# Last stages of layers 0 and 3: the sum over scan directions done band by band, with the norm, gate and projection of a band behind it

## What is computed

```python
# y: the four directions, each put back in the order of the pixels; D_skip weighs the input u
y = y_dir0 + y_dir1 + y_dir2 + y_dir3 + u * D_skip.sum(directions)
mu  = mean(y, over the 192 channels);  var = var(y, over the 192 channels)
y = (y - mu) * rsqrt(var + 1e-5) * ln_gamma + ln_beta
y = y * z                                   # z: the gate, computed earlier in the layer
x = x + y @ out_proj                        # 192 -> 96 channels, for each pixel
```

## Time and profile before

| what | value |
|---|---|
| median of 3 runs | 27758.6 us (27747.02 to 27776.92) |
| the profiled execution | 27776.42 us |
| its span in the trace | 27774.6 us |
| last stage of layer 0, sums (first to last, DVE) | 6959.6 to 7155.0 us |
| last stage of layer 0, steps (first matmul to last add) | 7155.1 to 7425.1 us |
| last stage of layer 3, sums | 27304.6 to 27500.0 us |
| last stage of layer 3, steps | 27500.1 to 27768.3 us |

### The profile page before, as it was taken

One profiled execution on the slowest core, in us unless ns is written; L12 is line 12 of the kernel. 1 busy time (PEld: TensorE's weight loads), 2 busy tenths in 40 slices (PEclk: granted clock), 3 DMA queues, 4 the chain that ended last, 5 costly groups with the idle time before them and its releaser, 6 DMA issues. The chain is left out here.

```text
span 27774.6 us, 412813 instructions
## 1 busy us (share of the span) xinstructions
PE 24946.7 (90%) x140112; PEld 9147.8 (33%) x140112; DVE 24955.1 (90%) x16019; ACT 14695.6 (53%) x19970; POOL 22628.6 (81%) x10100
## 2 busy tenths in 40 slices
PE   8989999999567999999987899999995899999996
PEld 3333333333233333333334333333332433333332
DVE  2489999999569999999986899999997799999997
ACT  1265555555267555555514655555552755555552
POOL 0179999999047999999971899999990599999992
PEclk9999999999677999999968999999997999999998
DMA  2242212221455212221266422212216622222224
GB/s 87 106 141 50 50 41 50 50 50 38 157 201 162 50 40 50 50 50 40 50 228 232 120 50 50 48 42 50 50 49 222 227 44 47 50 50 44 47 50 149
DMA packets 1121664, 2338.91 MB, mean 84 GB/s; under 512 B 98430, under 2 KB 609409, under 8 KB 1110893
## 3 DMA queue, kind: packets, MB, share of 16 engines
q1 hardware_dynamic: 1117748, 2309.42, 30.5%
q10 hardware_dynamic: 1728, 1.70, 0.0%
HBM read 1330.16 MB, written 980.58 MB: 83 GB/s over the span
## 5 line engine op out<-in xcount | busy, mean ns | idle before, releaser
L1598 POOL TENSOR_TENSOR scan_hc<-scan_bc,scan_h 128x1024 f32<-128x1024 f32 x6912 | 16131.4, 2384 | 135.7 <-PE scan_p_y L1710 72.1
L1786 DVE TENSOR_TENSOR_SCAN scan_h<-scan_da,scan_state,scan_dbu 128x1024 f32<-128x1024 f32 x6912 | 15948.4, 2332 | 38.6 <-POOL scan_dbu L1583 30.0
L1651 ACT ACTIVATE scan_da<-scan_da,scan_a_cur 128x1024 f32<-128x1024 f32 x6912 | 7521.7, 1088 | 6189.1 <-PE scan_da L1686 6188.7
L1686 PE MATMUL scan_da<-scan_dd,scan_ssel 32*128 32x512 f32 x27648 | 7870.4, 646 | 756.6 <-DVE scan_h L1786 40.8
L1686 PE MATMUL scan_p_du<-scan_dd,scan_ssel 32*128 32x512 f32 x27648 | 7906.8, 647 | 212.0 <-DMA scan_bc<-bc_d 110.0
L1773 DVE TENSOR_TENSOR scan_dbu<-scan_p_du,scan_bc 128x1024 f32<-128x1024 f32 x4752 | 5682.4, 1196 | 219.5 <-PE scan_p_du L1686 213.2
L1583 POOL TENSOR_TENSOR scan_dbu<-scan_bc,scan_dus 128x1024 f32<-128x1024 f32 x2160 | 5150.8, 2385 | 56.5 <-ACT scan_dus L1625 56.5
L1710 PE MATMUL scan_p_y<-scan_hc,scan_rsel 128*32 128x256 f32 x55296 | 4444.9, 393 | 0.0
L1694 PEld LDWEIGHTS scan_p_y<-scan_nought,scan_ssel 128*128 128x128 f32 x13824 | 2067.5, 189 | 4977.2 <-issue 3592.6
L1630 ACT ACTIVATE scan_state<-scan_h,scan_a_cur 128x1 f32<-128x1 f32 x6912 | 2036.9, 295 | 2734.3 <-DVE scan_h L1786 2610.6
L1686 PEld LDWEIGHTS scan_p_du<-scan_dd,scan_ssel 32*128 32x128 f32 x27648 | 2116.4, 185 | 4087.8 <-DVE scan_dbu L1773 3811.4
(11 more groups left out here) (225 smaller groups left out, 13731.3 us busy)
## 6 DMA issues: line engine op xcount, KB each, us to landing
scan_bc<-bc_d SPq DMA_DIRECT2D x576, 512.0 KB, 12.1
du_d<-prep_useq SPq DMA_DIRECT2D x384, 576.0 KB, 4.2
delta_d<-prep_delta SPq DMA_DIRECT2D x384, 576.0 KB, 4.7
y_d<-scan_y SPq DMA_DIRECT2D x576, 384.0 KB, 5.1
scan_dd<-delta_d SPq DMA_DIRECT2D x1136, 192.0 KB, 4.8
scan_dd<-du_d SPq DMA_DIRECT2D x1136, 192.0 KB, 6.5
fin_y<-y_d SPq DMA_DIRECT2D x288, 576.0 KB, 5.6
xs_d<-proj_xs_o SPq DMA_DIRECT2D x96, 588.0 KB, 3.3
```

What stands on the lines that cost most here:

```text
L1598: nc.gpsimd.tensor_tensor(hc[:, u % HC_SLOTS, :], c, h[:, u % H_SLOTS, :], ALU.mult).then_inc(hc_ready, 1)
L1651: nc.scalar.activation(da[u % DELTA_BANKS][:], da[u % DELTA_BANKS][:], ACT.Exp, scale=a_cur[:, slot(u)[0], u % UNITS:u % UNITS + 1]).then_ ...
L1686: return nc.tensor.matmul(dst[:, half * H:(half + 1) * H], ssel[rows, i, :], dd[rows, s, m, j, :], start=True, stop=True)
L1786: nc.vector.tensor_tensor_scan(h[:, v % H_SLOTS, :], da[v % DELTA_BANKS][:], dbu[:, v % DBU_SLOTS, :], state[:, v % UNITS:v % UNITS + 1], ...
```

## The change

Only `merge_finish_ln` is touched. The pieces are put in another order, and the steps run among them.

- `local` are the directions whose piece covers 12 whole lines of the image (a band: 1152 pixels of each tile); `whole` are those that walk by columns. In layer 0 all four are local. In layer 3 two are local and two whole.
- The pieces of the whole directions come first (`FIRST`: none in layer 0, 48 in layer 3). The local pieces follow band by band: in layer 0 there are `BAND` = 12 to a band, in layer 3 `BAND` = 6. There are 8 bands and 3 steps to a band (`PER_BAND`), so a turn of the DVE queue holds `TURN` = 4 pieces in layer 0 and 2 in layer 3.
- In turn t DVE adds the pieces of that turn, and then does `gate(s-2)`, `invert(s-1)`, `add(s-3)` with s = t - `LAG`, `LAG` = 3. PE no longer waits for all sums: before `centre_y` of every third step it waits for the band.
- SP issues, in each turn, the store, the loads of x and z, in every third turn of layer 0 a band of u, and then waits for each of the turn's pieces to be added in order to load the piece four further on.
- In layer 0 u is loaded and weighted in 8 bands of all three tiles (three ACT instructions of 1152 pixels each), two bands ahead; in layer 3 by tiles as before. The constants are loaded after the second load of u, ahead of all z and x; in layer 0 DVE waits for them before its first piece.
- Buffers: pieces 4 (were 6), z 3 (were 4), x 4 (were 6); the buffers of the steps have memory of their own.

```diff
-        DEEP = 4
-        X_DEEP = 6
+        DEEP = 3
+        X_DEEP = 4
...
-        Y_DEEP = 6
+        Y_DEEP = 4
...
+        whole = [k for k in range(DIRS) if walks[k][0] == "col"]
+        local = [k for k in range(DIRS) if walks[k][0] != "col"]
+        FIRST = [(m, k, c) for m in range(TILES) for k in whole for c in range(CHUNKS)]
+        BAND = TILES * len(local)
+        PIECES = FIRST + [(m, k, CHUNKS - 1 - b if walks[k][1] else b) for b in range(CHUNKS) for m in range(TILES) for k in local]
+        ALL = len(PIECES)
+        PER_BAND = DW // N
+        TURN = BAND // PER_BAND
+        LAG = 3
...
                 load_u(1)
-                for n in range(ALL - Y_DEEP):
-
-                    sp.wait_ge(added, (n + 1) * PAIRS + ONE)
-                    load_piece(n + Y_DEEP)
-                    if n == PER // 2:
-                        load_u(2)
...
+                for n in range(len(FIRST)):
+                    load_after(n)
+                    if n == CHUNKS:
+                        load_u(2)
                 for s in range(DEEP):
                     load_z(s)
                 for s in range(X_DEEP):
                     load_x(s)
...
+                for t in range(STEPS + 2 * LAG + 1):
+                    if t >= 2 * LAG + 1:
+                        store(t - 2 * LAG - 1)
+                    v = t - 2 * LAG - 2 + X_DEEP
                     if X_DEEP <= v < STEPS:
 
                         sp.wait_ge(stored[v % X_DEEP], 16 * (v // X_DEEP) + ONE)
                         load_x(v)
+                    v = t - 2 * LAG + DEEP
+                    if DEEP <= v < STEPS:
+
+                        sp.wait_ge(gated, (v - DEEP + 1) * TILES + ONE)
+                        load_z(v)
+                    if not whole and t % PER_BAND == 0 and t // PER_BAND + 2 < CHUNKS:
+                        load_u(t // PER_BAND + 2)
+                    for n in turn_pieces(t):
+                        load_after(n)
...
                 t.wait_ge(consts, 16 * 5 + ONE)
-                t.wait_ge(added, ALL * PAIRS + ONE)
                 for s in range(STEPS + 3):
...
                     if s < STEPS:
+                        if s % PER_BAND == 0:
+                            t.wait_ge(added, (len(FIRST) + (s // PER_BAND + 1) * BAND) * PAIRS + ONE)
                         centre_y(s)
...
                     if s >= 1:
                         deviation(s - 1)
+                    if not whole and s % PER_BAND == 0 and s // PER_BAND + 2 < CHUNKS:
+                        weigh(s // PER_BAND + 2)
                     if s < STEPS:
                         square(s)
...
+                for n in range(len(FIRST)):
+                    sum_piece(n)
                 d.wait_ge(consts, 16 * 5 + ONE)
-                for s in range(STEPS + 3):
+                for t in range(STEPS + 2 * LAG):
+                    for n in turn_pieces(t):
+                        sum_piece(n)
+                    s = t - LAG
                     if 0 <= s - 2 < STEPS:
                         gate(s - 2)
                     if 0 <= s - 1 < STEPS:
                         invert(s - 1)
```

More of the change, by code:

```diff
@@ L2149, in merge_finish_ln @@
         dskip_loaded = ph.sem("dskip_loaded")
-        u_loaded = [ph.sem(f"u_loaded{m}") for m in range(TILES)]
         piece_loaded = [ph.sem(f"piece_loaded{j}") for j in range(Y_DEEP)]
@@ L2156, in merge_finish_ln, with turn_pieces @@
         PAIRS = 2 if walks[0][0] == "window" or walks[0][2] == "snake" else 1
[L2157 to L2163, removed]
+        whole = [k for k in range(DIRS) if walks[k][0] == "col"]
[6 more added lines that the diff above has]
+        TURN = BAND // PER_BAND
+        U_PARTS = TILES if whole else CHUNKS
+        u_loaded = [ph.sem(f"u_loaded{i}") for i in range(U_PARTS)]
+        LAG = 3
+        def turn_pieces(t):
+            at = len(FIRST) + t * TURN
+            return range(at, min(at + TURN, ALL))
         z = ph.sb("z", [P, DEEP, TILES, N])
@@ L2171, in merge_finish_ln @@
         gamma = ph.sb("gamma", [P, P])
[L2173 to L2177, removed]
+        yc = ph.sb("yc", [P, 3, TILES, N])
+        sq = ph.sb("sq", [P, TILES, N])
+        yn = ph.sb("yn", [P, TILES, N])
+        t_ = [ph.sb(f"t{i}", [P, TILES, N]) for i in range(2)]
         sd = ph.sb("sd", [P, N])
@@ L2204, in load_piece, with load_u, load_after, load_z @@
                 def load_piece(n):
-                    m, k, c = where(n)
+                    m, k, c = PIECES[n]
                     at = (k * CHUNKS + c) * DW
                     sp.dma_start(y[:, n % Y_DEEP, :], y_d[:, m, at:at + DW]).then_inc(piece_loaded[n % Y_DEEP], 16)
-                def load_u(m):
-                    sp.dma_start(acc[:, m, :], u_d[:, m, :]).then_inc(u_loaded[m], 16)
+                def load_u(i):
+                    if whole:
+                        sp.dma_start(acc[:, i, :], u_d[:, i, :]).then_inc(u_loaded[i], 16)
+                    else:
+                        sp.dma_start(acc[:, :, i * DW:(i + 1) * DW], u_d[:, :, i * DW:(i + 1) * DW]).then_inc(u_loaded[i], 16)
+                def load_after(n):
+                    if n + Y_DEEP < ALL:
+                        sp.wait_ge(added, (n + 1) * PAIRS + ONE)
+                        load_piece(n + Y_DEEP)
+                def load_z(s):
+                    sp.dma_start(z[:, s % DEEP], z_d[:, :, s * N:(s + 1) * N]).then_inc(z_loaded[s % DEEP], 16)
+                def load_x(s):
+                    sp.dma_start(x[:, s % X_DEEP], x_d[:, :, s * N:(s + 1) * N].rearrange("b c n -> c b n")).then_inc(x_loaded[s % X_DEEP], 16)
+                def store(s):
+                    sp.wait_ge(out_ready, s + 1 + ONE)
+                    sp.dma_start(out_d[:, :, s * N:(s + 1) * N].rearrange("b c n -> c b n"),
+                                 x[:, s % X_DEEP]).then_inc(stored[s % X_DEEP], 16)
                 sp.dma_start(dskip[:], w["dskip"]).then_inc(dskip_loaded, 16)
@@ L2326, in square, with weigh @@
                     a.wait_ge(var_done, s + ONE)
-                    nc.scalar.activation(sq, yc[:, s % 3], ACT.Square).then_inc(squared, 1)
+                    nc.scalar.activation(sq[:], yc[:, s % 3], ACT.Square).then_inc(squared, 1)
+                def weigh(i):
+                    a.wait_ge(u_loaded[i], 16 + ONE)
+                    if whole:
+                        nc.scalar.activation(acc[:, i, :], acc[:, i, :], ACT.Copy, scale=dsum[:, i:i + 1]).then_inc(skip, 1)
+                    else:
+                        for m in range(TILES):
+                            own = acc[:, m, i * DW:(i + 1) * DW]
+                            nc.scalar.activation(own, own, ACT.Copy, scale=dsum[:, m:m + 1]).then_inc(skip, 1)
                 a.wait_ge(dsum_ready, 1 + ONE)
-                for m in range(TILES):
-                    a.wait_ge(u_loaded[m], 16 + ONE)
-                    nc.scalar.activation(acc[:, m, :], acc[:, m, :], ACT.Copy, scale=dsum[:, m:m + 1]).then_inc(skip, 1)
+                for i in range(TILES if whole else 2):
+                    weigh(i)
                 a.wait_ge(eps_set, 1 + ONE)
@@ L2351, in gate @@
                     d.wait_ge(gated, s * TILES + ONE)
-                    nc.vector.tensor_tensor(yn, yc[:, s % 3], p_r[:, :, 0:N], ALU.mult).then_inc(scaled, 1)
+                    nc.vector.tensor_tensor(yn[:], yc[:, s % 3], p_r[:, :, 0:N], ALU.mult).then_inc(scaled, 1)
                     d.wait_ge(scaled, s + 1 + ONE)
@@ L2369, in _, with sum_piece @@
                 nc.vector.tensor_reduce(dsum[:], dskip[:], mybir.AxisListType.X, ALU.add).then_inc(dsum_ready, 1)
-                for n in range(ALL):
-                    m, k, c = where(n)
+                def sum_piece(n):
+                    m, k, c = PIECES[n]
                     d.wait_ge(piece_loaded[n % Y_DEEP], (n // Y_DEEP + 1) * 16 + ONE)
-                    if n % PER == 0:
-                        d.wait_ge(skip, m + 1 + ONE)
+                    d.wait_ge(skip, m + 1 + (0 if whole else n // BAND * TILES) + ONE)
                     d.wait_ge(added, n * PAIRS + ONE)
```

4 lines of the change are left out of this document (removed).

## The result

The changed kernel takes 27612.9 us (median of 5 runs, 27607.63 to 27639.58) against 27762.16 us for the kernel before (5 runs): ratio 0.9943, 95% interval 0.9932 to 0.9955. That is 149 us less, where 156 were forecast. The forecast time was 27602, the range 27572 to 27667.

The account below looks back on a forecast made before the run. DVE would set layer 0's turn (14.1 us), the PE and ACT circle layer 3's step (10.35 us). Gains of 102 and 54 us sum to 156, against the median 27758.6 giving 27602 us, range 27572 to 27667.

Parts of the forecast that it names:

- DVE sets layer 0's turn: Layer 0's turns: DVE's sums 7.62 plus step work 6.47 make 14.1 us, over the PE circle's 10.35.
- Layer 0's fill: Start of layer 0: constants at 17.2 us, fifth piece at 33.7 (wait 8.9), turn 4 ends at 67.7.
- The 2.8 us for the short rows of z and x: Layer 0's start: extra transfer time before the fifth piece, as these rows go at 4.1 us per 1.18 MB.
- Layer 0's drain: Layer 0 after the last reciprocal at 333.7 us: 1.7, two circles (20.7), then 28.9 to last add at 385.0.
- from here PE sets the pace again: Layer 0 after `invert(19)`: `centre_y(21)` 1.7 us later, `centre_y(23)` two circles (20.7) on, last add 28.9 behind.
- rival 1: Layer 0's PE stays at 1.2 GHz, circle 17.1 us, 53 us lost over 18 turns (27655); chance 0.08.
- against it: Layer 0's PE clock: a slow turn has 3.7 us of idle to hide it; at the low rate no idle is left.
- rival 2: Transfers bound layer 0: each turn costs 16.1 us, 18 turns give back 36 us (27638); chance 0.06.
- The 12.7 us of the working: Layer 0's transfers for four pieces, a step and a third of a u band: 12.7 of 14.1 us, covered tightly.
- rival 3: Sums don't fit layer 3's loop: 2.92 us added to every circle, turns 3 to 23, lose 61 us (27663); chance 0.03.
- Layer 3's fill: Layer 3's start: column pieces 2.41 us each, waits 7.8 in FIRST, band 0 done at 163.0 us instead of 217.4.
- rival 4: SP's queue holds pieces back in both layers: 8.7 us a turn, 339 us, 182 slower in all (27941); chance 0.05.

Follow-up runs that it names:

- e2: Changed kernel with each step's reciprocal done twice on DVE, the first into a spare tile: 27696.98 us.
- e8: Changed kernel with loads reordered as in e6, plus the reciprocal root made on ACT (logarithm, exponential) instead of ACT's root and DVE's reciprocal: 27529.45 us, ratio 0.9913 to kernel before.
- e5: Changed kernel with 12 unread matmuls of 128 columns in PE's idle time ahead of each spread of layer 0 (steps 1 to 19): 27599.65 us.
- e9: The kernel of e6 again, timed in rounds against the kernel before: 27591.63 us, ratio 0.9935.
- e3: Kernel before the change with each step's reciprocal done twice on DVE: 27767.58 us.
- e4: Changed kernel with each turn's store one turn earlier in SP's queue, so SP waits for DVE's add before issuing that turn's piece loads: 27769.51 us.
- e6: Changed kernel with constants, first z and x behind the first pieces, layer 3's u in quarter tiles, layer 0's u bands later, two waits moved: 27589.48 us.

## Why the prediction was right, point by point

- **DVE sets layer 0's turn:** shown by the gapless DVE, by e2 (+2.4 us a turn for +2.5 us of work) and by e8 (-2.4 where nothing else waits). The turn is 13.8 us, not 14.1: `add` takes 0.89 us behind a reciprocal, not 0.95, and the sums, the reciprocal and the add are each followed by an instruction that begins some 0.08 us before their recorded end, so that adding durations counts too much. Over 18 turns that is 4.9 us.
- **Layer 0's fill:** the fifth piece came 34.5 us after the first load (33.7 forecast). The constants came later than forecast, 19.4 us after that load instead of 17.2, so the wait for the fifth piece was 7.5 us, not 8.9. The waits in turn 3 and ahead of turn 4 were mis-sized: 1.1 + 3.5 us instead of "about 1". Turn 4 ended at 72.3, not 67.7. This and the point above cancelled, by luck: the last reciprocal of the turns ended at 333.8 us, 333.7 forecast. (The 2.8 us for the short rows of z and x come to 2.7 by the prediction's own numbers, which changes nothing.)
- **Layer 0's drain:** 53.1 us instead of 51.3. PE enters it at the low clock, which the step "from here PE sets the pace again" left out. With a fast PE it is 50.3 us in e5 and 50.4 in e9. Which it is depends on whether the last turn was a slow or a fast one for PE.
- **PE's clock (rival 1)** fell as the rival said, to 0.86 over the turns, with `spread` at 3.22 us in the slow ones. It costs the turns nothing (e5). Both parts of "against it" were right: the slow turn is hidden, and it leaves PE so little idle time (0.65 us before the next `spread`) that the next turn is mostly fast again. So the whole turns at the low clock that the rival's 53 us need didn't come.
- **Transfers (rival 2)** were no bound in the changed kernel: share 0.79 over 7040 to 7263. The 12.7 us of the working is for a turn with its third of a u band. Of such turns the changed kernel has share 0.82 (7040.65 to 7165.3), 11.4 us of 13.85. So 12.7 was about a tenth too much. e8 shows the same from the other side, 11.7 us a turn with the share at 1.00.
- **Layer 3's steps (rival 3):** 10.35 us as before, the sums in the idle before `gate`, 0.45 us left of it (0.29 forecast). e3 shows the room that was there, e2 what happens when it is used up.
- **Layer 3's fill** is the term that was mis-sized most: first band at 168.0 us, not 163.0. Of the 5.0, 2.6 are the column pieces, 2.45 to 2.47 us each instead of 2.41; 0.9 are the two waits in FIRST (2.32 + 6.40 instead of 7.8); and 1.6 lie behind FIRST, where the pieces waited 10.27 us behind the first z and x, not 8.7.
- **SP's queue (rival 4)** doesn't hold pieces back, since the store waits for a turn that is over. In e4, where it is moved by one turn, DVE waits about as long as the rival said in layer 0, and in layer 3 hardly at all.

## What to carry to other kernels

When two phases of a stage load different engines, put the first between the instructions of the second and check three things by hand: the busy sum of the engine that gets both, the idle slot into which the new work must fit, and, in each issuing queue, what the wait ahead of every load is waiting for. A load's place in the queue is worth as much as the overlap: a store one turn too early cost 155 us in e4, and a reordering brought 41 to 43 us of stage time in e6 and e9. Once an engine sets the pace, try to move its work to one that doesn't slow it; here the reciprocal moved to ACT paid off, a third of the sums moved to POOL did not.

## What the runs showed that I had not expected

- POOL's adds made DVE's 1.6 times as long on average (954 to 1558 ns for the same 576 pixels), while POOL needed 2032 ns for one of its own. Moving a third of the sums made the turn 0.4 us longer.
- The busy share of the DMA engines followed the bytes closely: 0.82 at 291 GB/s in the changed kernel's turns with u, 1.00 at 346 GB/s in e8's (7017.3 to 7122.7). In time that is 11.4 and 11.7 us a turn. The share has to be taken over turns that load the same: over 7040 to 7263, where 7 of 16 turns load no u, it was 0.79 at 277 GB/s. The turns with u, in the changed kernel and in e8:

```profile
7040.65:7165.30 124.65, 105.38 (x418) 50.12 (x414) 120.74 (x128) 36.20 (x36) 0.00 (x0) 0.87 0.82 291
```

```profile
7017.30:7122.70 105.40, 95.68 (x415) 47.11 (x414) 99.68 (x118) 40.77 (x47) 0.00 (x0) 0.95 1.00 346
```

- The low clock of PE showed up as a cost only where PE set the pace again, in the drain, and there it was 2.8 us. PE doesn't stay slow: a slow turn leaves it so little idle time that the next is mostly fast.
